# Contracting the scan's states with C over blocks of 16 tokens in place of 32

## The chip, the cores and the metric

The kernel runs on one core of one Trainium2 chip. Its time is the device time of one execution in microseconds (us), here as the median of several runs. The engines of a core are TensorE (PE, with its weight loads as PEld), VectorE (DVE), ScalarE (ACT), GpSimd (POOL) and SyncE (SP, which only issues DMAs here). Each works through its own queue in program order; they wait for each other by semaphores.

## The reference, cut to what matters

Four layers follow each other on an image of 48 channels and 128x128 pixels. The change lies in the third, a selective scan over L = 4096 tokens with D = 192 features, each feature with 192 states:

```python
def step(h, inp):
    d_l, u_l, B_l, C_l = inp
    dA = jnp.exp(d_l[:, :, None] * A[None])
    h = dA * h + (d_l * u_l)[:, :, None] * B_l[:, None, :]
    y = jnp.einsum('bdn,bn->bd', h, C_l)
    return (h, y)
_, ys = jax.lax.scan(step, h0, xs)
```

So for each feature d and token l, y[d, l] is the sum over the 192 states n of h[d, n, l] times C[n, l].

## The kernel before, in words

`project_tokens` (L1347) first makes B, C and delta for all tokens and keeps B and C in SBUF with the states on partitions: `b0`, `c0` hold states 0 to 127; `b1` holds the other 64 states twice, on both halves of the partitions. `c_even` and `c_odd` hold the other 64 states of C on one half each, with zeros on the other half.

`scan` (L1618) takes the features in 32 groups of 6 and the tokens in 4 chunks of 1024, 128 chunks in all. A chunk has 9 slots: 6 for the first 128 states of the 6 features, and 3 in which two features share the partitions (states 128 to 191 of one on the lower half, of the other on the upper half). For each slot k:

- PE makes `du` (`delta_u`, L1731) and `keep` (`delta`, L1720), 2 matmuls of 512 columns in bf16 each, which spread a row of delta over the partitions. `du` has one PSUM buffer, `keep` has two, so `delta(k + 1)` waits until the recurrence of slot k - 1 is done (`wait_past(pe, state_ready, s - 1)`, L1725).
- ACT copies `du` to SBUF (`copy_du`, L1799) and takes the exponential of `keep` in place (`exponential`, L1806).
- POOL multiplies the copy by B (L1891).
- DVE runs the recurrence over the 1024 tokens as one scan instruction (`recur`, L1846; called R(k) below), which waits for POOL's product and for the exponential.

The contraction with C runs one chunk behind. Since C differs from token to token, PE multiplies a block of 32 tokens of C (stationary) by the states of the same 32 tokens of all features (moving); of each 32x32 product only the diagonal is wanted. `unit` (L1742) does this for 128 tokens: four blocks, each with its own 32 rows of PSUM, and three products for each (first 128 states, then `c_even` for the lower and `c_odd` for the upper half of the shared slots). DVE's `extract` (L1858) multiplies two units in PSUM by a mask that keeps the diagonals, PE's `select` (L1760) sums each block's 32 rows into one, ACT's `copy_y` (L1813) scales half a chunk into `y_sb`, and SP stores it.

The order on each queue is written by hand. PE, for slot k: `delta_u(k + 2)`, `delta(k + 1)`, `select` (even k from 2), `unit(k)` (k < 8). ACT: `copy_du(k + 2)`, `exponential(k + 1)`, and `copy_y` at slots 5 and 8. DVE: `extract` before R(2), R(4), R(6) and R(8). The waits of `unit` are

```python
if q == 0:
    pe.wait_ge(state_ready, (g * NCH + c + 1) * SLOTS)
if q % 2 == 0:
    wait_past(pe, extracted, (g * NCH + c) * (UNITS_Y // 2) + q // 2)
```

Of the kernel before, what the change touches and what calls it, by code (L numbers as in the profile page):

```python
# [1319 lines left out]
TB = 32  # L1320
UNIT = GD * TB
UNITS_Y = CH // P
# [5 lines left out]
def scan_layer(nc, image, gmean, norm, sems, ident, d, stats, kept_image, kept):  # L1328
# [14 lines left out]
def project_tokens(nc, image, gmean, norm, sems, d, b_c, parts, skip_rows, kept, stats):  # L1343
# [3 lines left out]
    with ExitStack() as ctx:  # L1347
# [98 lines left out]
        def _(pe):  # L1446
# [25 lines left out]
            def stats(i, first=False):  # L1472
                for k in range(4):
                    if not first:
                        pe.wait_ge(bc_copied, (i - 1) * 5 + (1, 2, 3, 5)[k])
# [18 lines left out]
        def _(act):  # L1494
# [123 lines left out]
def scan(nc, image, d, b_c, parts, y_rows, kept_image, returned):  # L1618

    with ExitStack() as ctx:  # L1620
# [4 lines left out]
        pick = n.sb("pick", [P, 4])  # L1625
        rows = n.sb("rows", [P, 2, CH], BF16)
        state_odd = n.sb("state_odd", [P, SLOTS, CH])
        y_sb = n.sb("y_sb", [P, 2, UNIT])
# [6 lines left out]
        masked = [room[SLOTS + 6][:, k * 2 * UNIT:(k + 1) * 2 * UNIT] for k in range(2)]  # L1635
# [43 lines left out]
        def _(sp):  # L1679
# [8 lines left out]
            def store(g, c, half):  # L1688
                sp.wait_ge(y_copied, (g * NCH + c) * 2 + half + 1)
                sp.nop(nofuse=True)  # L1690
                for q in range(4):
                    t0 = c * CH + half * BLK + q * P
                    dst = y_rows[ds(g * GD, GD), t0:t0 + P].rearrange("f (b t) -> b f t", t=TB)
                    sp.dma_start(dst, y_sb[32 * q:32 * q + 4, half, :].rearrange(
                        "b (f t) -> b f t", t=TB)).then_inc(y_stored[half], 16)

# [18 lines left out]
            for stored in y_stored:  # L1715
                sp.wait_ge(stored, NG * NCH * 64)

        @block.tensor
        def _(pe):
# [22 lines left out]
            def unit(g, c, q):  # L1742

                h = state[c % 2]
                w = (g * NCH + c) * UNITS_Y + q
# [4 lines left out]
                half_d = GD // 2  # L1750
                for stat, d0, d1, s0 in ((2, 0, GD, 0), (3, 0, half_d, GD), (4, half_d, GD, GD)):
                    for tb in range(4):
                        t0 = q * P + tb * TB
                        part = slice(tb * TB, (tb + 1) * TB)
                        out = y[part, (q % 2) * UNIT + d0 * TB:(q % 2) * UNIT + d1 * TB].rearrange("p (f t) -> p f t", t=TB)
                        last = nc.tensor.matmul(out, b_c[stat][:, c * CH + t0:c * CH + t0 + TB],  # L1756
                                                h[:, s0:s0 + d1 - d0, t0:t0 + TB], start=stat == 2, stop=stat == 4)
# [14 lines left out]
            def slot_steps(g, c, k, first=False):  # L1772

                if not (first and c == 0):
                    gy, cy = (g, c - 1) if c else (g - 1, NCH - 1)
                    if k % 2 == 0 and k >= 2:
                        select(gy, cy, k // 2 - 1)
                    if k < UNITS_Y:
                        unit(gy, cy, k)
# [14 lines left out]
            for k in range(SLOTS):  # L1794
                slot_steps(NG, 0, k)
# [847 lines left out]
```

## Time and profile before

| | |
|---|---|
| median of 3 runs | 7487.12 us (7486.96 to 7488.85) |
| the profiled execution | 7483.13 us, of which its span 7471.9 us |
| stage of the scan | 3735 to 6553 us of the span |
| busy in the whole span | DVE 90%, PE 81%, ACT 70%, POOL 46% |

A row of the timeline gives the start, the duration and the engine of one instruction or of several alike that follow each other (x2, x8). TensorE shows an fp32 matmul as two records, so one `unit` product of four blocks is a row of 8. Instructions of one engine overlap at their ends, so what one costs its engine is read from start to start, not from its duration.

### The profile page before, as it was taken

What the parts mean: (1) busy time and instruction counts of PE and PEld (TensorE: products, weight loads), DVE (VectorE), ACT (ScalarE), POOL (GpSimd) and SP (SyncE); (2) the same over time, 40 slices, a digit from 0 to 9 for tenths busy, and PEclk for the clock granted to TensorE, in tenths of its full rate; (3) what the DMA queues carried; (4) which work ended last, traced back from release to release, by engine and by line L of the source; (5) the groups of instructions that cost most, each with busy time, mean ns of one, the idle gap of its engine ahead of it and who ended that gap; (6) DMA issues with size and microseconds to landing.
All of it is one profiled execution on the core that took longest, in us unless ns stands there. A gap on an engine that the chain in (4) does not pass through costs nothing. (4 is left out here: it accounts for less than half of the span.)

```text
span 7471.9 us, 169388 instructions
## 1 busy us (share of the span) xinstructions
PE 6062.0 (81%) x69188; PEld 2635.0 (35%) x69188; DVE 6709.0 (90%) x5902; ACT 5234.7 (70%) x5319; POOL 3445.5 (46%) x1801
## 2 busy tenths in 40 slices
PE   6899999999999999897678888888888888866000
PEld 3433333333333333564233333333333333344000
DVE  8899999999999999798699999999999999964765
ACT  3488888888888888433588888888888888821000
POOL 2000000000000000000399999999999999925777
PEclk9999999999999999998899999999999999978555
DMA  3200000000000000000200000000000000032232
GB/s 66 56 12 9 10 9 9 12 9 10 9 9 12 9 10 6 7 7 11 71 6 6 6 6 6 6 6 6 6 6 6 6 6 6 6 90 56 78 80 71
DMA packets 146944, 153.65 MB, mean 21 GB/s; under 512 B 66540, under 2 KB 125708, under 8 KB 144924
## 3 DMA queue, kind: packets, MB, share of 16 engines
q1 hardware_dynamic: 120224, 89.43, 4.7%
q0 software_dynamic: 24576, 50.36, 2.6%
q8 instruction: 529, 8.67, 0.5%
q10 hardware_dynamic: 1440, 3.75, 0.3%
q14 instruction: 175, 1.43, 0.1%
HBM read 101.83 MB, written 37.95 MB: 19 GB/s over the span
## 5 line engine op out<-in xcount | busy, mean ns | idle before, releaser
L1891 POOL TENSOR_TENSOR k_image<-k_image,s_b 128x1024 f32<-128x1024 f32 x1152 | 2701.5, 2356 | 117.4 <-ACT k_image L1804 82.9
L797 ACT ACTIVATE att_prob<-att_scores,a_bound,a_temp 128x1024 f32<-128x1024 f32 x2048 | 2354.2, 1200 | 363.9 <-PE att_scores L747 363.9
L808 DVE TENSOR_TENSOR att_prob_lo<-att_prob 128x1024 f16<-128x1024 f32 x2048 | 2440.1, 1237 | 168.8 <-ACT att_prob L797 158.5
L732 POOL TENSOR_TENSOR k_image<-k_image,att_rden 48x512 f32 x32 | 68.6, 2142 | 2896.4 <-DVE att_rden L829 2896.4
L1804 ACT COPY k_image<-h_du 128x1024 f32<-128x1024 f32 x1152 | 1166.1, 1012 | 322.5 <-PE h_du L1738 322.3
L1854 DVE TENSOR_TENSOR_SCAN h_state_odd<-h_keep,k_image 128x1024 f32<-128x1024 f32 x576 | 1363.1, 2461 | 0.3 <-ACT h_keep L1810 0.3
L1810 ACT ACTIVATE h_keep<-h_keep,h_decay 128x1024 f32<-128x1024 f32 x1152 | 1256.7, 1091 | 75.3 <-PE h_keep L1727 51.6
L747 PE MATMUL att_scores<-att_queries,att_keys 32*128 32x512 f16 (+1 forms) x20480 | 1292.9, 377 | 19.5 <-DMA att_keys<-qk_halves 16.8
L764 PE MATMUL att_sums<-att_prob,a_values 128*64 128x512 bf16 x8192 | 1129.0, 396 | 0.0
L1727 PE MATMUL h_keep<-h_rows,h_spread 128*128 128x512 bf16 x2304 | 698.3, 385 | 513.2 <-DVE h_state_odd L1854 263.1
L1738 PE MATMUL h_du<-h_rows,h_spread 128*128 128x512 bf16 x2304 | 699.8, 385 | 35.2 <-DMA h_rows<-parts 33.2
L747 PEld LDWEIGHTS att_scores<-att_queries,att_keys 32*128 32x128 f16 (+1 forms) x20480 | 436.6, 93 | 792.0 <-ACT att_prob L797 408.5
L1854 DVE TENSOR_TENSOR_SCAN k_image<-h_keep,h_state_odd,k_image 128x1024 f32<-128x1024 f32 x288 | 681.5, 2461 | 0.0
L1854 DVE TENSOR_TENSOR_SCAN k_image<-h_keep,k_image 128x1024 f32<-128x1024 f32 x288 | 663.3, 2396 | 7.8 <-POOL k_image L1891 7.0
L2144 POOL DMA_INDIRECT b_shared<-cells,b_index x512 | 515.2, 1006 | 311.3 <-issue 154.9
L771 PE MATMUL att_sums<-att_prob_lo,a_values 128*64 128x512 f16 x4096 | 610.7, 378 | 0.0
L764 PEld LDWEIGHTS att_sums<-att_prob,a_values 128*64 128x64 f16 x8192 | 371.4, 108 | 671.1 <-ACT att_prob L797 408.0
L2199 PE MATMUL b_ps_o<-k_ident,b_passed 128*48 128x128 f32 x128 | 31.8, 403 | 596.3 <-issue 397.9
L1727 PEld LDWEIGHTS h_keep<-h_rows,h_spread 128*128 128x128 bf16 x2304 | 133.5, 97 | 1076.6 <-DVE h_state_odd L1854 488.3
L2328 DVE TENSOR_TENSOR b_prod<-b_shared,b_weight 128x768 f32<-128x768 f32 x128 | 123.0, 961 | 252.8 <-DMA b_shared<-cells,b_index 238.3
L1864 DVE TENSOR_TENSOR k_image<-h_y,h_diagonal 128x384 f32<-128x384 f32 x512 | 338.1, 660 | 8.8 <-PE h_y L1756 8.7
L1756 PE MATMUL h_y<-h_state_odd,s_c 128*32 128x192 f32 x4096 | 324.6, 336 | 1.8 <-DVE h_state_odd L1854 1.8
(309 smaller groups left out, 6563.2 us busy)
## 6 DMA issues: line engine op xcount, KB each, us to landing
y_rows<-h_y_sb SPq DMA_DIRECT2D x1024, 3.0 KB
att_queries<-qk_halves SPq DMA_DIRECT2D x124, 128.0 KB, 2.2
parts<-t_part SPq DMA_DIRECT2D x48, 192.0 KB, 2.5
h_rows<-parts SPq DMA_DIRECT2D x128, 72.0 KB
b_shared<-cells,b_index POOLq DMA_INDIRECT x512
qk_halves<-qkv_hi SPq DMA_DIRECT2D x128, 48.0 KB, 1.6
cells<-b_shared SPq DMA_DIRECT2D x4, 1536.0 KB, 5.1
att_keys<-qk_halves SPq DMA_DIRECT2D x32, 128.0 KB, 2.5
```

The lines of the kernel that those rows point to most:

```text
L747: last = nc.tensor.matmul(scores[:, (2 * n + r // 2) % SLOTS_S, r % 2 * BLK:(r % 2 + 1) * BLK], keys[part, j, g * KT:(g + 1) * KT], querie ...
L764: nc.tensor.matmul(sums[part, slot, :], values[:, key_tile(u, r), part], prob_hi[:, u % RING, r * BLK:(r + 1) * BLK], start=g == 0 and r = ...
L771: last = nc.tensor.matmul(sums[r * CHUNK:(r + 1) * CHUNK, slot, :], values[:, key_tile(u, r), 0:CHUNK], prob_lo[:, u % RING, r * BLK:(r + ...
L797: nc.scalar.activation(prob[:, u % RING, :], scores[:, u % SLOTS_S, :], ACT.Exp, bias=bound[:, 0:1], scale=temp[:, 0:1]).then_inc(prob_rea ...
L808: nc.vector.tensor_tensor(prob_lo[:, u % RING, :], prob[:, u % RING, :], prob_hi[:, u % RING, :], ALU.subtract).then_inc(low_ready, 1)
L1727: last = nc.tensor.matmul(keep[:, k % 2, cols], spread[:, 0, slot, :], rows[:, c % 2, cols], start=True, stop=True)
L1738: last = nc.tensor.matmul(du[:, cols], spread[:, 1, slot, :], rows[:, c % 2, cols], start=True, stop=True)
L1804: nc.scalar.copy(du_sb[k % 3], du[:, :]).then_inc(du_copied, 1)
L1810: nc.scalar.activation(keep[:, k % 2, :], keep[:, k % 2, :], ACT.Exp, scale=decay[:, ds(g * SLOTS + k // STEPS * SLOTS + k % SLOTS, 1)]).t ...
L1854: nc.vector.tensor_tensor_scan(out=state[c % 2][:, slot, :], data0=keep[:, k % 2, :], data1=drive[k % 3], initial=initial, op0=ALU.mult, o ...
L1891: nc.gpsimd.tensor_tensor(drive[k % 3], du_sb[k % 3], b[:, c * CH:(c + 1) * CH], ALU.mult).then_inc(drive_ready, 1)
L2144: nc.gpsimd.indirect_dma_start(got[:, y % GOT, k * CELL:(k + 1) * CELL], None, cells, bass.IndirectOffsetOnAxis(index[:, k, y:y + 1], 0)). ...
```

## The change

The blocks of tokens shrink from 32 to 16 (`TB`). Two blocks share 32 rows of PSUM: C is stored with 16 columns of zeros between every two blocks, so that the stationary operand is 32 columns wide, once [block | zeros] and once [zeros | block] (`e` in `products`), and the two products accumulate in the same place. All four units of half a chunk now fit in one PSUM bank; `extract` and `select` run twice for each chunk in place of four times, each on 384 columns. `c_even` and `c_odd` are gone: `c1` holds the upper states on both halves, and the product for the lower half of the shared slots (`unit_low`) and for the upper half (`unit_high`) each use 64 rows. The two are apart on PE's queue: slot k is now `delta_u(k + 2)`, `unit_low(k)`, `delta(k + 1)`, `unit_high(k)`, and then `select` at slots 4 and 8. `copy_y` handles 8 rows of 384 columns in place of 128 rows of 192, and the stores of half a chunk are one DMA in place of four. The core of the diff:

```diff
-TB = 32
+TB = 16
+HALF_UNITS = 4
+PAIRS = BLK // (2 * TB)
+PADDED = PAIRS * 3 * TB
+SECTIONS = BLK // (HALF_UNITS * TB)
...
-        b_c = [ln.sb(name, [P, L]) for name in ("b0", "b1", "c0", "c_even", "c_odd")]
+        b_c = [ln.sb(name, [P, L]) for name in ("b0", "b1")] + [ln.sb(name, [P, L // BLK, PADDED]) for name in ("c0", "c1")]
...
-            for k, t in enumerate((b_c[3][HALF_K:P, :], b_c[4][0:HALF_K, :])):
+            for k, t in enumerate((b_c[2], b_c[3])):
                 pool.wait_ge(cleared, 3 + k)
-                nc.gpsimd.memset(t, 0.0).then_inc(cleared, 1)
+                gaps = t[:, :, :].rearrange("p h (j e t) -> p (h j) e t", e=3, t=TB)[:, :, 1, :]
+                nc.gpsimd.memset(gaps, 0.0).then_inc(cleared, 1)
...
-                    if k < 3:
-                        nc.scalar.activation(b_c[k][:, ds(i * BLK, BLK)], ps_b[:, k, :], ACT.Identity,
-                                             bias=bias_bc[:, k:k + 1]).then_inc(bc_copied, 1)
+                    dst, src = b_c[k], ps_b[:, k, :]
+                    if k < 2:
+                        dst = dst[:, ds(i * BLK, BLK)]
                     else:
-                        for to, part_k in ((3, slice(0, HALF_K)), (4, slice(HALF_K, P))):
-                            nc.scalar.activation(b_c[to][part_k, ds(i * BLK, BLK)], ps_b[part_k, k, :], ACT.Identity,
-                                                 bias=bias_bc[part_k, k:k + 1]).then_inc(bc_copied, 1)
+                        dst = dst[:, ds(i, 1), :].rearrange("p h (j e t) -> p (h j) e t", e=3, t=TB)[:, :, 0:3:2, :]
+                        src = src.rearrange("p (e j t) -> p j e t", e=2, t=TB)
+                    nc.scalar.activation(dst, src, ACT.Identity, bias=bias_bc[:, k:k + 1]).then_inc(bc_copied, 1)
...
+            def products(g, c, q, stat, k, e, last):
+
+                h, half, u = state[c % 2], q // HALF_UNITS, q % HALF_UNITS
+                half_d = GD // 2
+                if stat == 2:
+                    d0, d1, s0 = 0, GD, 0
+                else:
+                    d0, d1, s0 = (half_d, GD, GD) if last else (0, half_d, GD)
+                for tb in range(4):
+                    t0 = half * BLK + (e * 4 + tb) * HALF_UNITS * TB + u * TB
+                    col = (tb * HALF_UNITS + u) * 3 * TB + e * TB
+                    out = y[tb * 2 * TB:(tb + 1) * 2 * TB, u * UNIT + d0 * TB:u * UNIT + d1 * TB]
+                    ins = nc.tensor.matmul(out.rearrange("p (f t) -> p f t", t=TB), b_c[stat][k, c * 2 + half, col:col + 2 * TB],
+                                           h[k, s0:s0 + d1 - d0, t0:t0 + TB], start=stat == 2 and e == 0, stop=last and e == 1)
+                return ins
+
+            def unit_low(g, c, q):
+
                 if q == 0:
                     pe.wait_ge(state_ready, (g * NCH + c + 1) * SLOTS)
-                if q % 2 == 0:
-                    wait_past(pe, extracted, (g * NCH + c) * (UNITS_Y // 2) + q // 2)
...
+                if q % HALF_UNITS == 0:
+                    wait_past(pe, extracted, (g * NCH + c) * 2 + q // HALF_UNITS)
+                for e in range(2):
+                    products(g, c, q, 2, slice(0, P), e, False)
+                wait_past(pe, unit_ready, (g * NCH + c) * UNITS_Y + q)
+                for e in range(2):
+                    ins = products(g, c, q, 3, slice(0, HALF_K), e, False)
+                ins.then_inc(unit_lower, 1)
+
+            def unit_high(g, c, q):
+
+                pe.wait_ge(unit_lower, (g * NCH + c) * UNITS_Y + q + 1)
+                for e in range(2):
+                    ins = products(g, c, q, 3, slice(HALF_K, P), e, True)
+                ins.then_inc(unit_ready, 1)
...
-                for j in range(2):
-                    q = (2 * i + j) % 4
-                    last = nc.tensor.matmul(picked[32 * q:32 * q + 4, 0:UNIT], pick[:, :],
-                                            masked[i % 2][:, j * UNIT:(j + 1) * UNIT], start=True, stop=True)
-                last.then_inc(selected, 1)
...
+                wait_past(pe, y_copied, e - 1)
+                nc.tensor.matmul(picked[32 * i:32 * i + SECTIONS, 0:HALF_UNITS * UNIT], pick[:, :], masked[i],
+                                 start=True, stop=True).then_inc(selected, 1)
...
             def group(g, first=False, last=False):
                 for k in range(STEPS):
                     if not last or k + 2 < STEPS:
                         delta_u(g, k + 2)
+                    slot_low(g, k // SLOTS, k % SLOTS, first)
                     if not last or k + 1 < STEPS:
                         delta(g, k + 1)
-                    slot_steps(g, k // SLOTS, k % SLOTS, first)
+                    slot_high(g, k // SLOTS, k % SLOTS, first)
...
-                if slot % 2 == 0 and slot >= 2 and not (first and c == 0):
+                if slot % HALF_UNITS == 0 and slot and not (first and c == 0):
                     gy, cy = (g, c - 1) if c else (g - 1, NCH - 1)
-                    extract(gy, cy, slot // 2 - 1)
+                    extract(gy, cy, slot // HALF_UNITS - 1)
```

`slot_low` calls `unit_low` for k < 8; `slot_high` calls `unit_high` for k < 8 and then `select(k // 4 - 1)` for k = 4 and 8.

## Rows read from the trace of the kernel before

**Rows 1.** Busy time of each engine in the stage of the scan.

```profile
3735.00:6553.00 2818.00, 2296.99 (x31231) 983.01 (x31229) 2803.96 (x1664) 2413.77 (x2559) 2701.47 (x1152) 1.00 0.03 7
```

The columns are PE, PEld, DVE, ACT and POOL busy (instructions), granted clock, DMA share, GB/s.

**Rows 2.** Waits of all engines, 3860 to 6500 us: total, times, longest.

```profile
PEld h_keep L1727 <- DVE h_state_odd L1854: 464.5, 484, 1.6
PEld h_keep L1727 <- DVE k_image L1854: 446.5, 481, 1.6
ACT k_image L1804 <- PE h_du L1738: 297.9, 844, 0.5
POOL k_image L1891 <- ACT k_image L1804: 62.1, 302, 0.3
ACT h_keep L1810 <- PE h_keep L1727: 46.0, 121, 0.4
```

**Rows 3.** Timeline of DVE over one chunk.

```profile
4998.49 2.45 DVE L1854 TENSOR_TENSOR_SCAN h_state_odd<-h_keep,k_image 128x1024 f32<-128x1024 f32 x1
5000.73 0.66 DVE L1864 TENSOR_TENSOR k_image<-h_y,h_diagonal 128x384 f32<-128x384 f32 x1
5001.18 4.71 DVE L1854 TENSOR_TENSOR_SCAN h_state_odd<-h_keep,k_image 128x1024 f32<-128x1024 f32 x2
...
5022.76 0.66 DVE L1864 TENSOR_TENSOR k_image<-h_y,h_diagonal 128x384 f32<-128x384 f32 x1
```

**Rows 4.** Timeline of all engines, 5006 to 5011 us.

```profile
5005.68 1.01 ACT L1804 COPY k_image<-h_du 128x1024 f32<-128x1024 f32 x1 [0.24 <-PE h_du L1738]
...
5006.12 2.47 DVE L1854 TENSOR_TENSOR_SCAN h_state_odd<-h_keep,k_image 128x1024 f32<-128x1024 f32 x1
5006.66 1.09 ACT L1810 ACTIVATE h_keep<-h_keep,h_decay 128x1024 f32<-128x1024 f32 x1
...
5007.68 0.32 ACT L1818 ACTIVATE h_y_sb<-h_picked 128x192 f32<-128x192 f32 x1
5007.89 1.01 ACT L1804 COPY k_image<-h_du 128x1024 f32<-128x1024 f32 x1
...
5008.38 4.70 DVE L1854 TENSOR_TENSOR_SCAN k_image<-h_keep,h_state_odd,k_image 128x1024 f32<-128x1024 f32 x2
...
5008.65 0.60 PE L1727 MATMUL h_keep<-h_rows,h_spread 128*128 128x512 bf16 x2 [1.06 <-DVE h_state_odd L1854]
...
5009.19 0.53 PE L1756 MATMUL h_y<-h_state_odd,s_c 128*32 128x192 f32 x8
5009.29 1.09 ACT L1810 ACTIVATE h_keep<-h_keep,h_decay 128x1024 f32<-128x1024 f32 x1 [0.40 <-PE h_keep L1727]
...
5009.54 0.35 PE L1756 MATMUL h_y<-h_state_odd,s_c_even 128*32 128x96 f32 x8
...
5009.70 0.35 PE L1756 MATMUL h_y<-h_state_odd,s_c_odd 128*32 128x96 f32 x8
...
5009.98 0.60 PE L1738 MATMUL h_du<-h_rows,h_spread 128*128 128x512 bf16 x2
```

**Rows 5.** Timeline of PE at a slot with `select`.

```profile
5013.14 0.60 PE L1727 MATMUL h_keep<-h_rows,h_spread 128*128 128x512 bf16 x2 [0.31 <-DVE k_image L1854]
...
5013.67 0.33 PE L1768 MATMUL h_picked<-k_image,h_pick 128*4 128x192 f32 x2
...
5013.70 0.36 PE L1756 MATMUL h_y<-h_state_odd,s_c 128*32 128x192 f32 x2
...
5013.83 0.33 PE L1768 MATMUL h_picked<-k_image,h_pick 128*4 128x192 f32 x2
```

**Rows 6.** Timeline of the scan's first slots, with a wait of DVE for ACT.

```profile
3736.39 13.87 POOL L1891 TENSOR_TENSOR k_image<-k_image,s_b 128x1024 f32<-128x1024 f32 x6 [18.02 <-ACT k_image L1804]
...
3740.49 1.10 ACT L1810 ACTIVATE h_keep<-h_keep,h_decay 128x1024 f32<-128x1024 f32 x1
...
3741.69 8.83 DVE L1854 TENSOR_TENSOR_SCAN k_image<-h_keep,k_image 128x1024 f32<-128x1024 f32 x4 [0.63 <-ACT h_keep L1810]
```

**Rows 7.** One line's instructions: duration in ns, least, median and most.

```profile
L1756 PE MATMUL h_y<-h_state_odd,s_c x4096: 326/326/531, 3782.9 to 6551.3; 128*32 128x192 f32 x196
L1756 PE MATMUL h_y<-h_state_odd,s_c_odd x4096: 246/246/368, 3783.4 to 6551.7; 128*32 128x96 f32 x196
```

**Rows 8.** Timeline of ACT in the projection, one block of 512 tokens.

```profile
3670.81 0.67 ACT L1524 ACTIVATE s_c<-t_ps_b,t_bias_bc 128x512 f32 x1
3671.38 0.67 ACT L1528 ACTIVATE s_c_even<-t_ps_b,t_bias_bc 64x512 f32 x1
3672.08 0.68 ACT L1528 ACTIVATE s_c_odd<-t_ps_b,t_bias_bc 64x512 f32 x1
3677.82 1.33 ACT L1506 ACTIVATE t_second<-t_once,t_bias_two 96x512 f32<-96x512 f32 x2 [5.06 <-DVE t_both L1582]
```

More of the change, by code:

```diff
@@ L1474, in stats @@
                     if not first:
-                        pe.wait_ge(bc_copied, (i - 1) * 5 + (1, 2, 3, 5)[k])
+                        pe.wait_ge(bc_copied, (i - 1) * 4 + k + 1)
                     pe.nop(nofuse=True)
@@ L1624, in scan @@
         diagonal = n.sb("diagonal", [P, TB])
-        pick = n.sb("pick", [P, 4])
+        pick = n.sb("pick", [P, SECTIONS])
         rows = n.sb("rows", [P, 2, CH], BF16)
         state_odd = n.sb("state_odd", [P, SLOTS, CH])
-        y_sb = n.sb("y_sb", [P, 2, UNIT])
+        y_sb = n.sb("y_sb", [P, HALF_UNITS * UNIT])
         room = [image[:, W + k * CH:W + (k + 1) * CH] for k in range(NPIX // CH)]
@@ L1634, in scan @@
         drive, du_sb = room[SLOTS:SLOTS + 3], room[SLOTS + 3:SLOTS + 6]
-        masked = [room[SLOTS + 6][:, k * 2 * UNIT:(k + 1) * 2 * UNIT] for k in range(2)]
+        masked = [room[SLOTS + 6][:, k * HALF_UNITS * UNIT:(k + 1) * HALF_UNITS * UNIT] for k in range(2)]
         spread_f = state_odd[0:ROWS_G, 0:2 * SLOTS * P // CH + 1, :].rearrange("p s t -> p (s t)")[:, 0:2 * SLOTS * P]
@@ L1690, in store @@
                 sp.nop(nofuse=True)
[L1691 to L1695, printed above, removed]
+                t0, run = c * CH + half * BLK, HALF_UNITS * TB
+                dst = y_rows[ds(g * GD, GD), t0:t0 + BLK].rearrange("f (r x) -> r f x", x=run)
+                src = y_sb[32 * half:32 * half + SECTIONS, :].rearrange("r (f x) -> r f x", x=run)
+                sp.dma_start(dst, src).then_inc(y_stored[half], 16)
             def group(g, first=False):
@@ L1715, in _ @@
             for stored in y_stored:
-                sp.wait_ge(stored, NG * NCH * 64)
+                sp.wait_ge(stored, NG * NCH * 16)
         @block.tensor
@@ L1746, in unit @@
+            def unit_low(g, c, q):
                 if q == 0:
                     pe.wait_ge(state_ready, (g * NCH + c + 1) * SLOTS)
-                if q % 2 == 0:
-                    wait_past(pe, extracted, (g * NCH + c) * (UNITS_Y // 2) + q // 2)
[L1750 to L1757, printed above, removed]
@@ L1758, in unit @@
-                last.then_inc(unit_ready, 1)
+                if q % HALF_UNITS == 0:
[6 more added lines that the diff above has]
+                ins.then_inc(unit_lower, 1)
@@ L1766, in select @@
-                for j in range(2):
-                    q = (2 * i + j) % 4
-                    last = nc.tensor.matmul(picked[32 * q:32 * q + 4, 0:UNIT], pick[:, :],
-                                            masked[i % 2][:, j * UNIT:(j + 1) * UNIT], start=True, stop=True)
-                last.then_inc(selected, 1)
[L1772 to L1779, printed above, removed]
+                wait_past(pe, y_copied, e - 1)
@@ new lines, in select, with behind, slot_low @@
+                nc.tensor.matmul(picked[32 * i:32 * i + SECTIONS, 0:HALF_UNITS * UNIT], pick[:, :], masked[i],
+                                 start=True, stop=True).then_inc(selected, 1)
+            def behind(g, c, first=False):
+                if first and c == 0:
+                    return None
+                return (g, c - 1) if c else (g - 1, NCH - 1)
+            def slot_low(g, c, k, first=False):
+                gc = behind(g, c, first)
+                if gc and k < UNITS_Y:
+                    unit_low(*gc, k)
@@ L1781, in group, with slot_high @@
+            def slot_high(g, c, k, first=False):
+                gc = behind(g, c, first)
+                if gc and k < UNITS_Y:
+                    unit_high(*gc, k)
+                if gc and k % HALF_UNITS == 0 and k:
+                    select(*gc, k // HALF_UNITS - 1)
             def group(g, first=False, last=False):
@@ L1794, in _ @@
             for k in range(SLOTS):
-                slot_steps(NG, 0, k)
+                slot_low(NG, 0, k)
+                slot_high(NG, 0, k)
         @block.scalar
@@ L1815, in copy_y @@
                 m = (g * NCH + c) * 2 + half
-                act.wait_ge(selected, 2 * m + 2)
-                wait_past(act, y_stored[half], (g * NCH + c) * 64)
-                nc.scalar.activation(y_sb[:, half, :], picked[:, 0:UNIT], ACT.Copy, scale=SIGMOID_1).then_inc(y_copied, 1)
+                act.wait_ge(selected, m + 1)
+                wait_past(act, y_stored[half], (g * NCH + c) * 16)
+                rows = slice(32 * half, 32 * half + SECTIONS)
+                nc.scalar.activation(y_sb[rows, :].rearrange("r (f u t) -> r u f t", u=HALF_UNITS, t=TB),
+                                     picked[rows, 0:HALF_UNITS * UNIT].rearrange("r (u f t) -> r u f t", f=GD, t=TB),
+                                     ACT.Copy, scale=SIGMOID_1).then_inc(y_copied, 1)
             def group(g, first=False, last=False):
@@ L1858, in extract @@
             def extract(g, c, i):
[L1860 to L1861 removed]
+                e = (g * NCH + c) * 2 + i
+                dve.wait_ge(unit_ready, (g * NCH + c) * UNITS_Y + (i + 1) * HALF_UNITS)
                 wait_past(dve, selected, e - 1)
                 split = "p (f t) -> p f t"
[L1864 to L1865 removed]
+                nc.vector.tensor_tensor(masked[i].rearrange(split, t=TB),
+                                        y[:, 0:HALF_UNITS * UNIT].rearrange(split, t=TB),
+                                        diagonal[:, :].unsqueeze(1).broadcast_to([P, HALF_UNITS * GD, TB]),
                                         ALU.mult).then_inc(extracted, 1)
             def slot_extract(g, c, slot, first=False):
[L1870 removed]
+                if slot % HALF_UNITS == 0 and slot and not (first and c == 0):
                     gy, cy = (g, c - 1) if c else (g - 1, NCH - 1)
[L1872 removed]
+                    extract(gy, cy, slot // HALF_UNITS - 1)
             def group(g, first=False):
@@ L2524, in constants @@
     diagonal = (place_in_block[:, None] % TB == np.arange(TB)[None, :]).astype(np.float32)
-    block_of = (place_in_block[:, None] // TB == np.arange(4)[None, :]).astype(np.float32)
+    section = place_in_block // TB % 2 * 4 + place_in_block // (2 * TB)
+    section_of = (section[:, None] == np.arange(SECTIONS)[None, :]).astype(np.float32)
     pick = np.zeros((C, 4, C, 4), np.float32)
@@ L2536, in constants @@
         "diagonal": diagonal,
-        "pick": block_of,
+        "pick": section_of,
         "w_pick": pick,
```

15 lines of the change are left out of this document (3 added, 12 removed).

## Prediction

> **What bounds the kernel now.** I first read the busy times by stage. The change lies in the scan's stage of 2818 us, where DVE is busy for 2804, POOL for 2701, ACT for 2414 and PE for 2297, with TensorE's clock at full [rows 1]. The waits say the same: DVE appears in none as a waiter; PE waits for DVE some 911 us before `keep` [rows 2]. So DVE sets the pace, and its timeline gives the price list. From one scan to the next it is 2.26 us (5006.12 to 5008.38 in [rows 4]); from a scan to an extraction 2.24, and from there to the next scan 0.45 (4998.49, 5000.73, 5001.18 in [rows 3]), though the records say 2.45 and 0.66. A chunk has 9 scans and 4 extractions: 5 x 2.26 + 4 x (2.24 + 0.45) = 22.06 us, and the same extraction does return after 5022.76 - 5000.73 = 22.03 us [rows 3]. 128 of these make the stage.
>
> The second thing to read is how near the next bound is. POOL alone needs (13.87 - 2.34) / 5 = 2.31 us for each slot [rows 6], where 2.34 is one product (2701 us over 1152) [rows 1], so 20.8 us a chunk. And there is a loop through four engines: R(k - 1) frees the `keep` buffer, PE fills it for slot k + 1, ACT takes the exponential, R(k + 1) uses it. Its pieces: a scan lasts 2.45; PE starts 0.06 after its end (5006.12 + 2.47 = 5008.59, start 5008.65); ACT starts 0.64 after PE (5009.29); the exponential takes 1.09 [rows 4]; DVE starts 0.10 after it (3740.49 + 1.10 = 3741.59, start 3741.69) [rows 6]. Together 4.34 us, against two scans of 4.52. **The slack is 0.18 us.** Whatever stands on PE's queue ahead of `keep` and starts only when a scan or an extraction is done costs DVE all of it but 0.18. In the kernel before nothing does: `unit` and its waits stand behind `keep`.
>
> **What the change removes.** DVE does 2 extractions in place of 4, each again 384 columns (I take the same price; runs of 16 in place of 32 elements are not in the trace, and I leave them at nothing). A chunk's DVE work is then 7 x 2.26 + 2 x 2.69 = 21.20 us, **0.86 us less**, and times 128 that is 110 us. POOL's 20.8 would still hide under this.
>
> **What it adds on PE.** Prices first. `keep` or `du`: 0.54 from start to the start of what follows (5008.65 to 5009.19), of which 2 x 0.22 is streaming (0.60 - 0.38 between the two) and 0.10 a gap at the change of tile shape. A `unit`: 0.16 for a round of four 192-column matmuls side by side, 0.08 for a round of 96 (5009.54 to 5009.70 for two), and a first weight load of 0.03 (5009.54 - 5009.19 - 2 x 0.16); the last two rounds end 0.12 before `du` starts (5009.98 - 5009.70 - 0.16) [rows 4]. No gap is seen where `select` and `unit` follow each other (5013.67, 5013.70), and both use 32-column tiles over all rows [rows 5]; so the gap belongs to the shape, not to the semaphore wait. A `select` pass of 192 columns takes 0.16 (5013.67 to 5013.83) [rows 5].
>
> The columns streamed stay the same (192 + 96 + 96 twice before; 4 rounds of 96 and 8 of 48 now), but the instructions double. I price a round of 48 columns at 0.04, half of 96, since loads are hidden at 0.08 and cost only about 0.03 where they are exposed; the other end is 0.08, the shortest round that the trace shows. For the gap between full-row and half-row products the trace has nothing: between 0 and the 0.17 by which a matmul's record outlasts its streaming (246 ns less 80; 326 less 160 [rows 7]). I take 0.12, the gap at the other shape changes. Then:
> - full-row products: 0.03 + 4 x 0.08 + 0.12 = 0.47
> - `low` and `high`: 0.03 + 4 x 0.04 + 0.12 = 0.31 each
> - `select`: two passes of 384 columns, 0.64 + 0.10 = 0.74, now twice a chunk and no longer side by side with a unit.
>
> A usual slot is 0.54 + 0.31 + 0.54 + 0.47 + 0.31 = 2.17 us of PE, under 2.26 by only 0.09. But the products in front of `keep` (0.47 + 0.31 = 0.78) are in three places not done early. Counting from the start of R(3):
>
> **A, slot 4.** `unit_low(4)` overwrites the columns that extraction 0 reads, and this extraction stands on DVE behind R(3): it ends at 2.24 + 0.66 = 2.90. PE starts at 2.96, `keep(5)` at 3.74, and R(5) can start at 3.74 + 0.64 + 1.09 + 0.10 = 5.57. Unhindered it would at 2.69 + 2.26 = 4.95. Lost: 0.62.
>
> **B, slot 5.** Behind `keep(5)` PE also has the select: 2.17 + 0.74 = 2.91, `keep(6)` at 6.65, R(6) at 8.48 and not 7.83. Lost: 0.65.
>
> **D, slot 6.** On ACT, `copy_y` takes 0.21 before the next copy starts (5007.68 to 5007.89); 192 columns more cost 0.16 at (1.01 - 0.32) / 832 us each, so 0.37. The exponential for R(6) starts at 6.65 + 0.64 = 7.29; `copy_y` 1.02 later (as 5006.66 to 5007.68), `copy_du` 0.37 after it, the next exponential 0.98 after that (as 5005.68 to 5006.66) [rows 4], at 9.66. R(7) starts at 9.66 + 1.09 + 0.10 = 10.85 and not 8.48 + 2.26 = 10.74. Lost: 0.11.
>
> **C, slot 0.** `unit_low(0)` needs all nine scans of the last chunk, so R(8), just as `keep(1)` does. It starts 0.06 after R(8) and holds `keep(1)` up by 0.78, of which 0.18 is slack. Lost: 0.60.
>
> After each, PE's 2.17 a slot suffices. Sum: 0.62 + 0.65 + 0.11 + 0.60 = 1.98 lost and 0.86 won: 1.12 us more for each of 127 chunks, **142 us more**. The profiled execution took 7483 us, so 7625; the median of the runs stands 4 us above it: **7629 us**.
>
> The Trainium skill, TensorEngine Tiling, section Key Properties, speaks against this change: it says that switching the tiling mode drains the engine, while changing the tile within a mode does not. The row agrees in kind, with 0.10 to 0.12 us and not the full 0.17. Taken as a full drain it gives the 7733 of the second case below.
>
> Costed at nothing: the projection, where one of ACT's three copies of C per block goes (0.67) but ACT then waits 5.06 us for DVE [rows 8]; the memsets, half as many elements on a POOL with time; the stores, fewer DMAs on a queue that nobody waits for [rows 2]. If cover were gone, the first would be worth 8 x 0.67 = 5 us. The last chunk's contraction has no `keep` between `low` and `high`, a few us either way.
>
> **The rivals.**
> 1. Waits as above, with the gap between half and full rows from 0 to 0.17. At 0 (A, B and C 0.12 less each): 0.76 a chunk, 7584.
> 2. A full drain of 0.17 at the four half-row boundaries of a slot: PE needs 2.41 > 2.26, and R(2), R(3), R(7) lose 0.15 each. A and C 0.12 more, B 0.24 more: 2.80 - 0.86 = 1.94 a chunk, 7733.
> 3. PE becomes the bound: a round of 48 columns costs 0.08. `low` and `high` are 0.47 each, a slot 2.49. A 0.78, B 0.97, C 0.76, and 0.23 at R(2), R(3), R(7): 3.20 - 0.86 = 2.34 a chunk, 7784. For it: twice the loads and matmuls. Against: 8 starts in 0.16 us show no floor [rows 4].
> 4. The other side: PE's work in front of `keep` is far cheaper than 0.78, say because half-row products run beside full-row ones. The waits then cost what exceeds 0.18; with none of them DVE's gain stands alone, 7487 - 110 = 7377. It decides where the work falls below about 0.45 us (each of three waits under 0.29). For it: PE is idle before `keep` for 0.31 [rows 5] to 1.06 us [rows 4], so the room is there on average. Against: in A and C the work cannot use that room, since it starts with the event that ends it.
> 5. The gain and the waits cancel within 0.2%.
>
> **How the numbers follow.** Case 1 has 0.60 (own range 7584 to 7700), case 2 0.12, case 3 0.12, case 4 0.10, case 5 0.04, dearer than 7790 0.02. The forecast is case 1's 7629. The range from 7560 to 7790 leaves out cases 4 and 5 and the last: 0.16. This kernel's runs differ by 0.03%, and 0.2% (15 us) is about what a measurement can tell from no change. Faster 0.10, same 0.04, slower 0.86.
>
> **What would show it.** The scan's stage lasts about 2960 us; DVE waits for ACT's exponential some 1.9 us a chunk, in front of R(1), R(5) and R(6) above all, and the busy time of its extractions halves to about 170 us. On PE, `keep(1)` and `keep(5)` start about 0.84 us after R(8) and the extraction end. Wrong would be: no idle time of DVE at these slots (case 4), equal waits at all slots (case 3), or rounds of 48 columns starting other than 0.04 us apart. POOL as the releaser of scans would overturn the whole.

## The result, and the profile after

| | before | after |
|---|---|---|
| median of 4 runs each, same chip | 7487.04 us (7485.34 to 7488.85) | 7603.65 us (7601.84 to 7608.53) |
| the profiled execution | 7483.13 us, span 7471.9 | 7604.4 us, span 7594.2 |
| last scan of DVE ends at | 6541.7 us | 6647.2 us |

The ratio is 1.0159 (95%: 1.0146 to 1.0172): the changed kernel is slower by 117 us, where 142 were forecast. The time lies inside the range. The scan's stage starts at 3735 us in both. Its scans end 105.5 us later, the contraction of the last chunk, which follows them, takes 12 us more, and the next stage starts at 6673.3 us in place of 6556.8, 116.5 later. Behind that, the two profiled executions took 915 and 921 us; these 6 us are not in the medians, which are 117 apart.

The busy times of the scan's stage after (PE, PEld, DVE, ACT, POOL, each with its instructions; granted clock, DMA share, GB/s), to be set against [rows 1]:

```profile
3735.00:6675.00 2940.00, 2412.58 (x53255) 1114.47 (x54272) 2729.48 (x1409) 2445.39 (x2560) 2683.29 (x1155) 0.99 0.03 7
```

DVE's busy time has fallen by 74 us and the stage is 122 us longer: DVE now stands still for 210 of 2940 us, where before it did for 14 of 2818. Most of that is seen in the waits (the view of [rows 2], 3860 to 6600 us, which is 120.6 chunks):

```profile
ACT h_keep L1841 <- PE h_keep L1731: 323.5, 531, 1.4
POOL k_image L1926 <- ACT k_image L1835: 214.2, 362, 1.2
...
DVE k_image L1888 <- ACT h_keep L1841: 87.7, 180, 0.6
DVE h_state_odd L1888 <- ACT h_keep L1841: 83.3, 182, 0.5
```

DVE was in none of these rows before. Now it waits 362 times for the exponential, three times a chunk, and ACT's own wait for PE's `keep` has grown from 46 to 324 us. POOL waits for ACT 214 us, and nobody waits for POOL: the other bound that the prediction named has not come into play. The groups of instructions by line (count, then busy us and mean ns of one, then idle time before) show that the extractions are down to 242 and 129 us, two a chunk, where four stood before:

```profile
L1898 DVE TENSOR_TENSOR k_image<-h_y,h_diagonal 128x384 f32<-128x384 f32 x242 | 128.6, 531 | 0.0
```

Where the three waits lie is read from DVE's timeline (as [rows 3]), from an extraction ahead of R(8) over the whole next chunk:

```profile
5030.50 0.53 DVE L1898 TENSOR_TENSOR k_image<-h_y,h_diagonal 128x384 f32<-128x384 f32 x1
5030.95 2.28 DVE L1888 TENSOR_TENSOR_SCAN k_image<-h_keep,k_image 128x1024 f32<-128x1024 f32 x1
5033.15 2.32 DVE L1888 TENSOR_TENSOR_SCAN h_state_odd<-h_keep,k_image 128x1024 f32<-128x1024 f32 x1
5035.90 6.83 DVE L1888 TENSOR_TENSOR_SCAN h_state_odd<-h_keep,k_image 128x1024 f32<-128x1024 f32 x3 [0.42 <-ACT h_keep L1841]
5042.65 0.53 DVE L1898 TENSOR_TENSOR k_image<-h_y,h_diagonal 128x384 f32<-128x384 f32 x1
5043.10 2.34 DVE L1888 TENSOR_TENSOR_SCAN h_state_odd<-h_keep,k_image 128x1024 f32<-128x1024 f32 x1
5045.84 2.35 DVE L1888 TENSOR_TENSOR_SCAN h_state_odd<-h_keep,k_image 128x1024 f32<-128x1024 f32 x1 [0.40 <-ACT h_keep L1841]
5048.73 4.60 DVE L1888 TENSOR_TENSOR_SCAN h_state_odd<-h_keep,k_image 128x1024 f32<-128x1024 f32 x2 [0.54 <-ACT h_keep L1841]
5053.25 0.53 DVE L1898 TENSOR_TENSOR k_image<-h_y,h_diagonal 128x384 f32<-128x384 f32 x1
```

The first scan is R(8) of the chunk before, which an extraction precedes. Then R(0) starts at 5033.15 and R(1) 2.75 later: place C. R(4) starts at 5043.10 and R(5) 2.74 later: place A. R(6) follows after another 2.89: place B. An undisturbed scan gives way to the next after 2.24 to 2.26 us, so the three cost 0.51, 0.49 and 0.65. R(7), between 5048.73 and 5053.25, loses nothing that one can read here. The same extraction returns after 22.75 us. This stretch begins with a short step of 2.20 (5030.95 to 5033.15), which the one in [rows 3] does not have; the next stretch without it lasts 22.80 (5053.25 to 5076.05), against 22.03 there. The short steps are those of the first chunk of each group of features, in both kernels; the loop through PE does not get shorter with them, so that such chunks lose a little more. Over all chunks the mean went from 21.90 to 22.72, and 0.82 x 128 = 105 us.

The timeline of all engines over the places A and B, cut to the chain from the extraction to R(6):

```profile
5042.65 0.53 DVE L1898 TENSOR_TENSOR k_image<-h_y,h_diagonal 128x384 f32<-128x384 f32 x1
...
5043.23 0.84 PE L1758 MATMUL h_y<-k_image,s_c 128*32 128x96 f32 x32 [1.24 <-DVE k_image L1898]
...
5044.23 0.38 PE L1731 MATMUL h_keep<-h_rows,h_spread 128*128 128x512 bf16 x1 [0.16 <-issue]
...
5044.54 0.38 PE L1758 MATMUL h_y<-k_image,s_c 64*32 64x48 f32 x16
...
5044.65 1.09 ACT L1841 ACTIVATE h_keep<-h_keep,h_decay 128x1024 f32<-128x1024 f32 x1 [1.43 <-PE h_keep L1731]
...
5044.84 0.81 PE L1787 MATMUL h_picked<-k_image,h_pick 128*8 128x384 f32 x2
...
5047.12 0.38 PE L1731 MATMUL h_keep<-h_rows,h_spread 128*128 128x512 bf16 x1 [0.16 <-issue]
...
5047.54 1.09 ACT L1841 ACTIVATE h_keep<-h_keep,h_decay 128x1024 f32<-128x1024 f32 x1 [0.30 <-PE h_keep L1731]
5048.55 0.47 ACT L1850 ACTIVATE h_y_sb<-h_picked 8x384 f32<-8x384 f32 x1
5048.92 0.98 ACT L1835 COPY k_image<-h_du 128x1024 f32<-128x1024 f32 x1
5049.81 1.06 ACT L1841 ACTIVATE h_keep<-h_keep,h_decay 128x1024 f32<-128x1024 f32 x1
```

The extraction ends at 5043.18 and `unit_low(4)` starts 0.05 later. Of the two matmuls of `keep(5)` the trace has lost the record of the first; the second starts at 5044.23, so the first did 0.22 earlier, at 5044.01. The products ahead of it took 0.78, as worked out. ACT starts 0.64 after it, ends at 5045.74, and R(5) starts 0.10 later. Then `unit_high`, the select (0.75), `du` and `unit_low(5)` stand in front of `keep(6)`, which comes 2.89 after `keep(5)`; 2.91 were forecast. `copy_y` takes 0.37 of ACT (5048.55 to 5048.92), also as forecast.

### The profile page after: what moved, and what is told of

It is laid out like the page before. It is cut to its first block and busy times, and to the rows that moved or that the text cites. A ratio compares the mean times of both kernels' runs of the same rounds, so it can differ in the third digit from the quotient of the medians.

```text
span 7594.2 us, 211668 instructions
## 1 busy us (share of the span) xinstructions
PE 6179.4 (81%) x91211; PEld 2768.6 (36%) x92228; DVE 6630.5 (87%) x5646; ACT 5260.1 (69%) x5311; POOL 3426.2 (45%) x1801
## 5 line engine op out<-in xcount | busy, mean ns | idle before, releaser
L1888 DVE TENSOR_TENSOR_SCAN h_state_odd<-h_keep,k_image 128x1024 f32<-128x1024 f32 x576 | 1330.2, 2337 | 87.8 <-ACT h_keep L1841 87.8
L1758 PE MATMUL h_y<-h_state_odd,s_c 128*32 128x96 f32 (+1 forms) x24576 | 626.7, 224 | 129.1 <-DVE k_image L1898 74.1
L1758 PE MATMUL h_y<-k_image,s_c 128*32 128x96 f32 (+1 forms) x24576 | 622.6, 223 | 125.2 <-DVE k_image L1898 79.4
L1888 DVE TENSOR_TENSOR_SCAN k_image<-h_keep,h_state_odd,k_image 128x1024 f32<-128x1024 f32 x288 | 665.1, 2337 | 43.9 <-ACT h_keep L1841 43.9
L1731 PE MATMUL h_keep<-h_rows,h_spread 128*128 128x512 bf16 x1288 | 468.4, 381 | 252.4 <-issue 163.8
L1758 PEld LDWEIGHTS h_y<-h_state_odd,s_c 128*32 128x32 f32 (+1 forms) x24576 | 413.1, 107 | 644.6 <-PE h_y L1758 215.9
L1758 PEld LDWEIGHTS h_y<-k_image,s_c 128*32 128x32 f32 (+1 forms) x24576 | 410.4, 107 | 642.5 <-PE h_y L1758 216.8
```

Source lines behind the costliest of these rows:

```text
L1758: ins = nc.tensor.matmul(out.rearrange("p (f t) -> p f t", t=TB), b_c[stat][k, c * 2 + half, col:col + 2 * TB], h[k, s0:s0 + d1 - d0, t0:t ...
L1888: nc.vector.tensor_tensor_scan(out=state[c % 2][:, slot, :], data0=keep[:, k % 2, :], data1=drive[k % 3], initial=initial, op0=ALU.mult, o ...
```

## The experiments

The first four ran on one chip, on which the kernel before took 7481.37 us (median of 13 runs); the last two on another, where it took 7433.37 (7 runs). Compared is by the ratio to the kernel before on the same chip; the changed kernel stands at 1.0159.

**Keep first.** In every slot `delta(k + 1)` goes back in front of the contraction. This tells whether the order on PE's queue, and not the finer products as such, costs the time.

```diff
                         delta_u(g, k + 2)
-                    slot_low(g, k // SLOTS, k % SLOTS, first)
                     if not last or k + 1 < STEPS:
                         delta(g, k + 1)
+                    slot_low(g, k // SLOTS, k % SLOTS, first)
                     slot_high(g, k // SLOTS, k % SLOTS, first)
```

> The changed kernel with one swap on PE's queue: `delta(k + 1)` stands ahead of `unit_low(k)`, as the unit stood behind it in the kernel before; everything else stays. Order theory: what costs time is that the products stand in front of `keep` at the slots where they start late, so the waits in front of R(1), R(5) and most of R(6) go (0.48 + 0.49 + most of 0.63 us a chunk). `unit_high` now follows `unit_low` directly and waits until it has drained, about 0.13 us more of PE a slot: 0.54 + 0.47 + 0.31 + 0.13 + 0.31 + 0.54 = 2.30 us against DVE's 2.26, so up to 0.3 us a chunk may stay at slot 6. Time: 7487 - 104 (DVE's shorter chunk) + 12 (the end of the stage) + 0 to 40 = 7395 to 7435. Rival, PE throughput: the doubled number of small products and tile shapes makes PE the bound, whatever the order; with 2.30 us a slot and the drains it stays at 7600 or above.

Measured: 7470.91 us (10 runs), ratio 0.9986 (0.9977 to 0.9996). DVE's timeline and PE's, each over a few slots:

```profile
5028.14 4.58 DVE L1888 TENSOR_TENSOR_SCAN h_state_odd<-h_keep,k_image 128x1024 f32<-128x1024 f32 x2
5033.09 4.59 DVE L1888 TENSOR_TENSOR_SCAN h_state_odd<-h_keep,k_image 128x1024 f32<-128x1024 f32 x2 [0.37 <-ACT h_keep L1841]
```

```profile
5020.90 0.60 PE L1731 MATMUL h_keep<-h_rows,h_spread 128*128 128x512 bf16 x2
5021.44 1.30 PE L1758 MATMUL h_y<-k_image,s_c 128*32 128x96 f32 x48
...
5023.18 0.60 PE L1731 MATMUL h_keep<-h_rows,h_spread 128*128 128x512 bf16 x2
```

The waits before R(1) and R(5) are gone, so A and C are due to the order. But R(4) and R(5) now take 5033.09 - 5028.14 = 4.95 us where two scans take 4.51: R(6) is 0.44 late. R(2) is 0.15 late. PE's slot is the reason: 5020.90 to 5023.18 is 2.28, 0.02 above DVE's 2.26, so that PE has nothing left to make good the select (0.75) before the next `keep`. The mean chunk is 21.73 us, 0.17 less than before, so most of DVE's gain of 0.86 is used up. The expectation was right in the mechanism, but the time lies 36 us above the upper end of its range, since I took PE to catch up.

**Slot 0 back.** The same swap in slot 0 alone.

```diff
-                    slot_low(g, k // SLOTS, k % SLOTS, first)
+                    back = k % SLOTS == 0
+                    if not back:
+                        slot_low(g, k // SLOTS, k % SLOTS, first)
                     if not last or k + 1 < STEPS:
                         delta(g, k + 1)
+                    if back:
+                        slot_low(g, k // SLOTS, k % SLOTS, first)
```

> The changed kernel with the swap at slot 0 alone: `keep(1)` stands ahead of `unit_low(0)`. Simple wait theory: the wait of 0.48 us in front of R(1) goes and nothing comes in its place, 7604 - 61 = 7543. Order theory by its own sums: between `keep(1)` and `keep(2)` PE now has two lows, 0.54 + 0.78 + 0.13 + 0.31 + 0.54 + 0.78 = 3.08 us against 2.26, so R(2) waits about 0.54 us (0.82 less a slack of 0.28) and nothing is won: 7604 to 7615, with the wait moved from R(1) to R(2).

Measured: 7608.58 us (7603.97 to 7612.48), ratio 1.017 (1.0153 to 1.0187), no different from the changed kernel. DVE's timeline from R(0) on:

```profile
5034.61 4.57 DVE L1892 TENSOR_TENSOR_SCAN h_state_odd<-h_keep,k_image 128x1024 f32<-128x1024 f32 x2
5039.67 4.59 DVE L1892 TENSOR_TENSOR_SCAN h_state_odd<-h_keep,k_image 128x1024 f32<-128x1024 f32 x2 [0.49 <-ACT h_keep L1845]
```

R(1) follows R(0) without a stop, and R(2) is late instead: 5.06 us for the two in place of 4.50. Whatever is shifted in one slot stands before `keep(2)` in the next. C can't be removed alone.

**High products late.** If the trouble is work that starts with DVE's last event and stands in front of `keep`, then what stands there should be work whose data are old. Slot k becomes `delta_u(k + 2)`, `unit_high(k - 1)`, `delta(k + 1)`, `select`, `unit_low(k)`; `slot_low` and `slot_high` change places in `group`, and with them:

```diff
             def slot_low(g, c, k, first=False):
+                if gc and k % HALF_UNITS == 0 and k:
+                    select(*gc, k // HALF_UNITS - 1)
                 if gc and k < UNITS_Y:
                     unit_low(*gc, k)
             def slot_high(g, c, k, first=False):
-                if gc and k < UNITS_Y:
-                    unit_high(*gc, k)
-                if gc and k % HALF_UNITS == 0 and k:
-                    select(*gc, k // HALF_UNITS - 1)
+                if gc and 1 <= k <= UNITS_Y:
+                    unit_high(*gc, k - 1)
```

> The changed kernel with another order on PE's queue for slot k: `delta_u(k + 2)`, `unit_high(k - 1)`, `delta(k + 1)`, `select`, `unit_low(k)`. The lower products stand behind `keep`, the upper ones, which wait for nothing late, fill the gap in front of it, and `du` or `keep` lies between the two halves, so no drain is waited for: 2.17 us of PE a slot. Price: the unit is done later, so each of the two extractions starts about 0.2 us late. Order theory: 7487 - 104 + 12 + 0.4 x 127 = 7446, in any case under 7487. PE throughput: at or above 7600.

Measured: 7431.66 us (7425.43 to 7435.15), ratio 0.9931 (0.9914 to 0.9948): faster than the kernel before. DVE's timeline:

```profile
5029.90 0.56 DVE L1898 TENSOR_TENSOR k_image<-h_y,h_diagonal 128x384 f32<-128x384 f32 x1 [0.17 <-PE h_y L1758]
5030.37 8.82 DVE L1888 TENSOR_TENSOR_SCAN k_image<-h_keep,k_image 128x1024 f32<-128x1024 f32 x4
5039.36 0.56 DVE L1898 TENSOR_TENSOR k_image<-h_y,h_diagonal 128x384 f32<-128x384 f32 x1 [0.16 <-PE h_y L1758]
```

No scan waits for an exponential any more. What is left is the extraction, which waits for `unit_high(3)` and `unit_high(7)`, one slot late now, for 0.17 us each.

**Before, with the unit first.** The rule put to the kernel before: its old products of 32 tokens, but placed ahead of `keep`.

```diff
                         delta_u(g, k + 2)
+                    slot_steps(g, k // SLOTS, k % SLOTS, first)
                     if not last or k + 1 < STEPS:
                         delta(g, k + 1)
-                    slot_steps(g, k // SLOTS, k % SLOTS, first)
```

> The kernel before (blocks of 32, zero-filled halves, four extractions) with one swap: `select` and `unit(k)` stand ahead of `delta(k + 1)`. No halves, no doubled products, PE needs 1.9 us a slot. Order theory: at slots 2, 4 and 6 `keep` starts 0.95 us after the extraction (select and unit), 3.78 us after the start of the scan before, so the scan after next starts at 5.61 in place of 4.95: 0.66 each; slot 8 0.14, slot 0 0.79 - 0.28 = 0.51. Together 2.6 us a chunk, 7487 + 334 = about 7820. Rival, that the loss comes from the halves and the doubled products: 7487, no change.

Measured: 7955.2 us (7953.81 to 7960.61), ratio 1.0635 (1.0617 to 1.0653), 135 us more than expected. DVE's timeline with R(0) of one chunk and two scans of it that follow each other, and two windows of the stage (columns as in the first view):

```profile
5014.77 2.35 DVE L1854 TENSOR_TENSOR_SCAN k_image<-h_keep,h_state_odd,k_image 128x1024 f32<-128x1024 f32 x1 [0.83 <-ACT h_keep L1810]
...
5025.82 2.34 DVE L1854 TENSOR_TENSOR_SCAN k_image<-h_keep,h_state_odd,k_image 128x1024 f32<-128x1024 f32 x1
5028.88 2.35 DVE L1854 TENSOR_TENSOR_SCAN k_image<-h_keep,h_state_odd,k_image 128x1024 f32<-128x1024 f32 x1 [0.72 <-ACT h_keep L1810]
```

```profile
3735.00:7020.00 3285.00, 2280.38 (x30674) 1074.38 (x31186) 2871.43 (x1663) 2341.38 (x2556) 2688.16 (x1152) 0.95 0.02 6
...
5008.00:5013.00 5.00, 3.29 (x35) 1.16 (x35) 4.29 (x4) 3.65 (x4) 3.91 (x3) 0.88 0.00 0
```

From the one scan to the next, here from R(4) to R(5), it is now 3.06 us, 0.80 more than 2.26. So the order alone slows the kernel, without one finer product. More was lost than expected, at two kinds of place. Behind R(2), R(4) and R(6) the work ahead of `keep` took longer than I had summed: 0.66 was expected for the 0.80, and the clock is not the reason, since it is 1.00 from 5025 to 5030 us. As an estimate, 3 x 0.14 x 127 makes 53 of the 135 us. Behind R(8) and R(0) the step differs from chunk to chunk: from R(8) to R(0) it is 3.17 us at 5011.60 and 2.44 at 5037.36, where 2.40 was expected. There the clock comes in: it is at 1.00 before [rows 1], but 0.95 over this stage and 0.88 from 5008 to 5013 us, so PE worked at the lower of its two levels, 1.2 GHz, for a part of the time. PE was busy for a smaller share of the stage than before, 69% against 82%. How the other 82 us divide between the clock and my sums for these two slots I can't say.

**High products mixed.** As high late, but the high products of units 3 and 7, for which the extraction waits, directly behind their low ones (the diff is against high late):

```diff
             def slot_low(g, c, k, first=False):
...
                     unit_low(*gc, k)
+                if gc and k % HALF_UNITS == HALF_UNITS - 1:
+                    unit_high(*gc, k)
             def slot_high(g, c, k, first=False):
-                if gc and 1 <= k <= UNITS_Y:
+                if gc and k % HALF_UNITS and k <= UNITS_Y:
                     unit_high(*gc, k - 1)
```

> The order of `high_late`, but the upper product of units 3 and 7, for which an extraction waits, follows its lower product at once and pays the drain of 0.13 us; the other six stay in the gap ahead of `keep`. Order theory: the 0.21 us that each of the two extractions lost in `high_late` comes back, PE still has under 2.26 us a slot, and slot 5 (keep 0.54, select 0.74, low 0.78, du 0.54, high 0.31 = 2.91) just meets its due time. A chunk falls from 21.43 to 21.01 us, DVE's own work: 7432 - 0.42 x 127 = 7378, and DVE waits nowhere regularly. Rival: POOL (20.8 us a chunk) or the drain takes over before that; then it stays at 7400 or above, with DVE waiting for POOL or for the exponential of slot 4 or 8.

Measured: 7339.84 us (7336.88 to 7340.95), ratio 0.9873 (0.9856 to 0.9889), 93.5 us less than the kernel before. DVE's timeline over one chunk:

```profile
5031.25 0.53 DVE L1900 TENSOR_TENSOR k_image<-h_y,h_diagonal 128x384 f32<-128x384 f32 x1
5031.69 9.06 DVE L1890 TENSOR_TENSOR_SCAN h_state_odd<-h_keep,k_image 128x1024 f32<-128x1024 f32 x4
5040.68 0.53 DVE L1900 TENSOR_TENSOR k_image<-h_y,h_diagonal 128x384 f32<-128x384 f32 x1
...
5052.38 0.53 DVE L1900 TENSOR_TENSOR k_image<-h_y,h_diagonal 128x384 f32<-128x384 f32 x1
```

The chunk takes 21.13 us here and 21.09 on the mean, 0.81 less than before: nearly all of the 0.86 that two extractions cost. DVE's waits are gone, for POOL as for the exponential, so the rival of the expectation, that POOL or the drain takes over, did not come. Expected were 109 us less than the kernel before.

**High mixed, the image returned later.** The end of the stage had grown by 12 us. PE's timeline of the changed kernel and of high mixed, after the last scan:

```profile
6647.29 7.69 PE L1758 MATMUL h_y<-h_state_odd,s_c 128*32 128x96 f32 x191 [1.18 <-DVE h_state_odd L1888]
6661.31 0.23 PE L1758 MATMUL h_y<-h_state_odd,s_c 64*32 64x48 f32 x1 [6.33 <-issue]
```

```profile
6434.12 6.69 PE L1758 MATMUL h_y<-h_state_odd,s_c 128*32 128x96 f32 x191 [1.45 <-DVE h_state_odd L1890]
6447.16 0.23 PE L1758 MATMUL h_y<-h_state_odd,s_c 64*32 64x48 f32 x1 [6.35 <-issue]
```

Both stop for 6.3 us before one last small matmul, and wait for nothing that the profile shows. In the changed kernel the window of 6650 to 6655 us says what else goes on:

```profile
6650.00:6655.00 5.00, 4.71 (x131) 3.18 (x128) 0.00 (x0) 0.00 (x0) 0.00 (x0) 0.50 1.03 138
```

All DMA engines are busy with the transfer of the kept image, which ACT issues when the last scan is done. The edit lets it wait for the last chunk's products too:

```diff
-            act.wait_ge(unit_ready, (NG * NCH - 1) * UNITS_Y)
+            act.wait_ge(unit_ready, NG * NCH * UNITS_Y)
```

> `high_mixed`, and ACT starts the two transfers that bring the kept half of the image back only after the last unit of the last chunk. In the changed kernel PE stands still for 6 to 7 us in the middle of that chunk's contraction, with no wait that the profile names, while these transfers fill the DMA engines. Theory that PE's instructions queue behind them: the pause goes, and the contraction of the last chunk takes some 16 us in place of 23. The transfers (14 us) then start about 16 us later, so the whole may gain up to 6 us or lose as much. Rival, that the pause comes from the half-row products themselves: it stays.

Measured: 7343.65 us (7341.26 to 7344.23), ratio 0.9879 (0.9862 to 0.9895), the same as without it. PE's timeline at the same place:

```profile
6432.04 7.70 PE L1758 MATMUL h_y<-h_state_odd,s_c 128*32 128x96 f32 x192 [1.45 <-DVE h_state_odd L1890]
6440.43 0.81 PE L1787 MATMUL h_picked<-k_image,h_pick 128*8 128x384 f32 x1 [0.68 <-DVE k_image L1900]
```

The pause is gone: it came with the transfer. The last `copy_y` starts 7.6 us earlier (6451.51 in place of 6459.13), and yet the next stage starts 2.3 us later, at 6463.86 in place of 6461.55. What holds it back are the last two stores of y, for which SP waits at the end of the stage. They are issued at 6450.92 and 6452.06, behind the transfer, and the view of the DMA queues has none of their packets from 6452 to 6460.7 us and all 112 of them after that; they land by 6463.4. In high mixed the last store, issued at 6459.68 with the transfer long done, lands 1.4 us later. So what the contraction gained was lost on the stores.

## Why the prediction was right

**What bounds the kernel.** Right. Before, DVE never waited; after, it waits for the exponential alone. The slower loop through PE took over at three places, and POOL did not.

**The 0.86 saved on DVE.** Right: extraction to scan is still 0.45, a slot with one 2.69, one without 2.26. High mixed gets 0.81 of it.

**PE's prices.** Right to 0.02 us. The slot pace, from PE's timeline between two `keep`:

```profile
5013.94 0.38 PE L1731 MATMUL h_keep<-h_rows,h_spread 128*128 128x512 bf16 x1 [0.16 <-issue]
...
5016.09 0.38 PE L1731 MATMUL h_keep<-h_rows,h_spread 128*128 128x512 bf16 x1 [0.16 <-issue]
```

It is 2.15 us, 2.17 forecast. The gap where a 512-column matmul of `keep` gives way to a 48-column one is 5044.54 - 5044.23 - 0.22 = 0.09 us. That leaves no room for the full drain of case 2 (2.41) or for rounds of 48 columns at 0.08 (2.49): both fell, and so did the other side, as the work ahead of `keep` was 0.78 and not below 0.45. By the Trainium skill (TensorEngine Tiling, Key Properties) a switch of the tiling mode drains the engine; the trace agrees that a switch costs something and has 0.09 us for it, not the 0.17 at which case 2 priced a full drain.

**A and C: the mis-sized terms.** Forecast 0.62 and 0.60, measured 0.49 and 0.51. The failed step is "a scan lasts 2.45" in the loop, and the extraction's end at "2.24 + 0.66". After the change a scan's record lasts 2.32 to 2.35 us and an extraction's 0.53, while the time from start to start is what it was. PE is released at the end of these, and still starts 0.05 to 0.06 after it, so it is released 0.12 earlier: the loop is 4.22 and not 4.34, the slack 0.30 and not 0.18. I took the durations at 5000 us of a trace in which DVE never stands still (see the last section), and carried them over to a kernel in which it does.

**B and D.** B was forecast at 0.65 and measured 0.65. D was forecast at 0.11 and measured 0.01: `copy_y` took its 0.37, but the copy behind it gave way to the exponential after 0.89 and not 0.98 (5048.92 to 5049.81).

**The sum.** 0.51 + 0.49 + 0.65 + 0.01 = 1.66 lost and 0.86 won is 0.80 a chunk against 1.12 forecast; the mean chunk shows 0.82. Times 128 it is 105 us and not 142. Each lost term is read against an undisturbed step of 2.24 to 2.26, so it is good to 0.02.

**The last chunk.** Said to be "a few us either way", measured 12 more. It starts when the scans end and costs all it lasts: 6.3 us are the pause beside the transfer. That is not the whole: with the pause gone (the return experiment) the contraction still takes 20 us, against 12 before. Of the rest no run tells how it divides; twice the matmuls, a granted clock of 0.50 (1.2 GHz) for a part of them (the window above; the kernel before had 0.87 over its last contraction), and extractions and selects that no longer lie beside products all point the same way.

Two errors of opposite sign, -37 and +12, make the 25 us between forecast and result. That they cancel in part is luck.

**The signs named beforehand.** The stage lasts 2940 us (2960 named), DVE waits in front of R(1), R(5) and R(6) and for ACT alone, and `keep(5)` starts 0.83 us after the extraction's end (0.84 named). The waits as the profile counts them are 171 us in 120.6 chunks, 1.4 a chunk and not 1.9. The extractions' busy time is 129 us there, 136 over the stage and not 170, since that number was the record of 0.66 us, which is 0.53 after.

That the order did it is shown, not only argued, by three runs: the order alone slows the kernel before (1.0635), taking it back removes A and C (0.9986), and an order in which only old data stand ahead of `keep` makes the same products faster than the kernel before (0.9873).

## What to carry to other kernels

When an edit moves work on a queue, ask for each instruction now ahead of the critical one *when its inputs are ready*: work on old data fits into the idle time of its engine, work released by the same event that releases the critical instruction adds its whole length but the slack. A saving on the bound engine is paid out only as far as the slack of the next loop goes, and that loop is best summed from start to start, piece by piece. Here finer blocks were worth 1.3%, but only with the low products behind `keep` and six of the eight high products of a chunk one slot later.

## What the hardware showed unexpectedly

**In the kernel before, DVE's records grow longer as the stage goes on.** From start to start nothing changes, but the end drifts. DVE's timeline of the kernel before, early and late in the stage and, for the scan and extraction, to be set against 2.45 and 0.66 in [rows 3]:

```profile
3899.05 2.34 DVE L1854 TENSOR_TENSOR_SCAN h_state_odd<-h_keep,k_image 128x1024 f32<-128x1024 f32 x1
3901.29 0.55 DVE L1864 TENSOR_TENSOR k_image<-h_y,h_diagonal 128x384 f32<-128x384 f32 x1
3901.74 4.60 DVE L1854 TENSOR_TENSOR_SCAN h_state_odd<-h_keep,k_image 128x1024 f32<-128x1024 f32 x2
...
6239.06 0.72 DVE L1864 TENSOR_TENSOR k_image<-h_y,h_diagonal 128x384 f32<-128x384 f32 x1
```

Two instructions that follow each other overlap by 0.10 us at 3899, by 0.21 at 5000 and by 0.27 at 6239; from about 5500 us on it grows no more. In the changed kernel, where DVE stops three times a chunk, the overlap is still 0.08 to 0.10 at 5000 us. Whoever waits for the end of such an instruction is released by so much later: `keep` starts 0.06 after the scan's recorded end at 3901.45 as at 5008.65, which is 2.40 us after the scan's start there and 2.53 here. Why the end drifts is open. That it takes a DVE without a pause is not shown: the profile lists no wait of DVE for high mixed either, and there an extraction lasts 0.53 at 5031 us and through the whole stage. Its starts are not quite even, though; from R(0) to R(1) it can take 0.13 more than 2.24.

**PE can stand still beside a large transfer** without a wait of its own: 6.33 and 6.35 us with the transfer, 6.63 in keep first, 5.94 in slot 0 back and 7.14 in high late, and none in the return experiment, where the transfer comes later. The view of the DMA queues (packets, MB, share of 16 engines) shows what was late. In the changed kernel, the queue of the transfer from 6642 to 6658 us, in which no packet of the queue named instruction is moved, and that queue from 6658 to 6662 us:

```profile
q10 hardware_dynamic: 112, 1.57, 65.7%
...
q8 instruction: 1, 0.02, 2.6%
```

In the changed kernel's stage such a packet of 16 KB comes every 4 to 10 us; here 17.4 us pass from 6640.8 to 6658.2. It took 1.7 us, and PE goes on 1.4 us after its end, at 6661.31. The other four kernels with a pause have the same gap ahead of one such packet, and PE goes on 1.4 to 1.6 us after its end; in the return experiment these packets come every 5 to 8 us around the contraction, and PE doesn't stop. So the traces support the reading that PE ran out of instructions while their transfer stood behind the large one. They don't say for which engine a packet is.
